# Gates and feature transposes of the last chunks spread among other products, and the last three weight blocks loaded in chained pieces

## What is computed

```python
x = x + attn(layernorm(x))      # z, h~ = projections; h = scan of (1-z) h + z h~ ; gate(h) * h
x = x + xattn(layernorm(x), ctx)  # 16 heads, 77 keys, softmax, Wo
x = x + ffn(layernorm(x))       # experts, below
```

```python
gate_scores = xf @ gate_W + gate_b                 # 4 experts
topk_scores, topk_idx = jax.lax.top_k(gate_scores, 2)
weights = jax.nn.softmax(topk_scores, axis=-1)
# expert e: layernorm2(relu(layernorm1(xf @ W1[e] + b1[e])) @ W2[e] + b2[e])
out = sum_k weights[k] * expert[topk_idx[k]](xf)   # + xf
```

## Time and profile before

| | us |
|---|---|
| timed, median of 3 | 1216.72 |
| timed, lowest and highest | 1214.84, 1219.3 |
| the profiled execution, whole | 1209.59 |
| its span | 1207.8 |

### The profile page before, as it was taken

One profiled execution on the slowest core, in us unless ns is written; L12 is line 12 of the kernel. 1 busy time (PEld: TensorE's weight loads), 2 busy tenths in 40 slices (PEclk: granted clock), 3 DMA queues, 4 the chain that ended last, 5 costly groups with the idle time before them and its releaser, 6 DMA issues.

```text
span 1207.8 us, 24523 instructions
## 1 busy us (share of the span) xinstructions
PE 1159.6 (96%) x6041; PEld 978.9 (81%) x6042; DVE 924.9 (77%) x2196; ACT 731.5 (61%) x2114; POOL 457.2 (38%) x410
## 2 busy tenths in 40 slices
PE   6999999999989999999999998989999999999993
PEld 5788888888878888888888877867888888888882
DVE  6888888887766677877868777678777777777774
ACT  5323333233486757767677662567777777777773
POOL 4040000000052314535445164357655555555543
PEclk9999999999999999999999998899999999999998
DMA  8754544444520302133021358885554444444433
GB/s 271 230 160 160 188 176 146 174 156 165 199 84 1 105 10 97 44 107 104 10 97 44 131 131 227 270 221 122 81 88 81 85 79 86 80 85 80 85 64 42
DMA packets 83237, 143.90 MB, mean 119 GB/s; under 512 B 20460, under 2 KB 24752, under 8 KB 82309
## 3 DMA queue, kind: packets, MB, share of 16 engines
q1 hardware_dynamic: 63872, 101.60, 25.8%
q0 software_dynamic: 18464, 39.14, 17.1%
q10 hardware_dynamic: 837, 2.41, 0.6%
HBM read 78.83 MB, written 67.83 MB: 121 GB/s over the span
## 4 chain that ended last, share of the span: by engine, by line
PE 83%; DMA 5%; DVE 4%; issue 3%; ACT 3%; POOL 2%; POOLq 0%; DVEq 0%; SPq 0%; ACTq 0%
PE banks L1097 27%; PE banks L681 21%; PE banks L746 7%; PE banks L891 6%; PE banks L879 5%; DMA out<-rows,scatter_rows 4%; PE banks L848 3%; PE banks L865 3%; PE banks L1109 2%; PE banks L907 2%; PE banks L1125 2%; ACT rows L1310 2%; PE banks L719 1%; PE banks L800 1%; PE banks L765 1%
## 5 line engine op out<-in xcount | busy, mean ns | idle before, releaser
L1097 PE MATMUL banks<-operands 128*128 x1608 | 388.6, 396 | 10.5 <-DVE operands L1570 5.2
L1097 PEld LDWEIGHTS banks<-operands 128*128 128x128 f32 x1608 | 298.1, 189 | 73.6 <-issue 7.4
L681 PE MATMUL banks<-operands 128*128 128x512 f32 (+2 forms) x1224 | 292.6, 394 | 3.5 <-DVE operands L1570 3.5
L681 PEld LDWEIGHTS banks<-operands 128*128 128x128 f32 (+1 forms) x1224 | 225.6, 192 | 47.8 <-DVE operands L1570 3.7
L1570 DVE TENSOR_TENSOR operands<-banks,operands 128x512 fp32r<-128x512 f32 (+3 forms) x328 | 217.7, 682 | 42.5 <-ACT operands L1189 38.8
L1189 ACT ACTIVATE operands<-banks 128x512 fp32r<-128x512 f32 (+3 forms) x328 | 191.7, 608 | 96.7 <-PE banks L879 45.0
L1310 ACT ACTIVATE rows<-banks,score_shift 128x77 f32<-128x77 f32 x512 | 162.7, 374 | 28.0 <-DVE score_shift L1792 27.2
L1189 ACT ACTIVATE operands<-rows 128x512 fp32r<-128x512 f32 (+3 forms) x79 | 55.3, 709 | 163.8 <-DVE rows L1641 138.1
L1495 ACT ACTIVATE banks<-banks,param_cols 128x128 f32<-128x128 f32 x268 | 99.2, 430 | 82.5 <-PE banks L1125 82.5
L2576 POOL DMA_INDIRECT out<-rows,scatter_rows x67 | 106.6, 1591 | 104.2 <-DVE rows L2315 65.1
L1310 ACT ACTIVATION_READ_ACCUMULATOR rows<-banks,score_shift 128x1 f32 x512 | 129.1, 256 | 0.0
(11 more groups left out here) (178 smaller groups left out, 1707.0 us busy)
## 6 DMA issues: line engine op xcount, KB each, us to landing
expert_parts<-operands SPq DMA_DIRECT2D x32, 512.0 KB, 3.0
operands<-expert_parts SPq DMA_DIRECT2D x8, 2048.0 KB, 11.1
rows<-in_x SPq DMA_DIRECT2D x8, 1024.0 KB, 5.4
rows<-in_L_ffn_W SPq DMA_DIRECT2D x32, 256.0 KB, 3.5
x_rows<-rows SPq DMA_DIRECT2D x8, 1024.0 KB, 4.3
rows<-x_rows SPq DMA_DIRECT2D x8, 1024.0 KB, 5.7
xf_rows<-rows SPq DMA_DIRECT2D x32, 256.0 KB, 2.7
out<-rows SPq DMA_DIRECT2D x32, 256.0 KB, 2.5
```

The lines of the kernel that those rows point to most:

```text
L681: last = nc.tensor.matmul(dst, stationary(a, k), moving(b, k), start=(t == 0 and k == 0), stop=(t == len(terms) - 1 and k == n_k - 1))
L1097: last = nc.tensor.matmul(dst, stationary[:, a, k, :], weights[:, w, bass.ds(e, 1), a2, k, :].rearrange("p e f -> p (e f)"), start=False, ...
```

## The change

On TensorE the gate scores of chunk 6 are cut in three (tile 0, tile 1, tiles 2 and 3) and stand between halves of the first projection of chunk 7; the scores of chunk 7 are cut in two and stand inside `first_product(3)` and `second_product(1)`; the position products move into `first_product(4)`. Both first banks are primed early, and ScalarE fills both at once; banks are given out anew so that this is free. `rows_in` of tile 2 and tile 3 and the transposes of the last two row groups of chunk 7 change places. The routing steps of chunk 7 on VectorE stand one tile later, `plan_early(1)` stands behind `read_positions`, and on GpSimd all eight scatters of chunk 5 stand ahead of `ln3_pow`. On SP block 3 is no longer loaded ahead of the last chunk's stores but together with block 2 behind them; `expert_in(2)` stands behind four pairs of tables; and blocks 5, 6 and 7 are loaded in 16 pieces of 128 KB, each of 64 partitions, every one waiting for the landing of the one before, with tables in between.

```diff
+            PIECES = 4 * KC
+            def load_expert_parts(s, parts):
+                e, w = s // 2, s % 2
+                for n in parts:
+                    a, k, rows = n // (2 * KC), n // 2 % KC, slice(n % 2 * (P // 2), (n % 2 + 1) * (P // 2))
+                    need(sp, w_in[s], 16 * n)
+                    sp.dma_start(weights[rows, w, e, a, k, :].bitcast(F32), ws_d[s, a, k, rows]).then_inc(w_in[s], 16)
...
             load_slot_pairs(3, 5)
-            load_expert(3)
             for j in range(2, TPC):
                 store_base(last - 1, j, slot3(last - 1)[:, j, :])
+            expert_in(1)
...
             load_rows(g2_rows, "L0_ffn_g2", g2_in)
-            expert_in(1)
-            load_slot_pairs(5, 7)
             load_expert(2)
-            load_slot_pairs(7, 9)
+            load_expert(3)
+            load_slot_pairs(5, 9)
             for s in range(2, 5):
                 expert_in(s)
             for s in range(5, 2 * NE):
-                load_expert(s)
-                load_slot_pairs(2 * s - 1, min(2 * s + 1, EARLY // 2))
+                for half_n in range(2):
+                    pair = 2 * s - 1 + half_n
+                    load_expert_parts(s, range(PIECES // 2 * half_n, PIECES // 2 * (half_n + 1)))
+                    load_slot_pairs(pair, min(pair + 1, EARLY // 2))
                 expert_in(s)
...
             last_turn(last)
-            for j in range(TPC):
+            project(last, tail, 0, (0, 1))
+            gate_scores(tail, (1,))
+            project(last, tail, 0, (2, 3))
+            pe.wait_ge(plan_ready, 1)
+            first_experts = [expert_at(pe, i) for i in range(3)]
+            gate_scores(tail, (2, 3))
+            for j in range(1, TPC):
                 project(last, tail, j)
             positions(last - 1, tail, "r")
-            pe.wait_ge(plan_ready, 1)
-            first_product(0, 0, expert_at(pe, 0))
+            first_product(0, 0, first_experts[0])
             for j in range(2):
                 xf_to_features(last, tail, j)
-            pe.wait_ge(mm_read, mm_num(tail, "o3") + 1)
-            prime(m1_bank[1])
-            first_product(1, 1, expert_at(pe, 1))
+            first_product(1, 1, first_experts[1])
+            rows_in(1, 0)
...
+            def prime_and_gates():
+                pe.wait_ge(b_t_read, t_num(tail, "xf3") + 1)
+                prime(m2_bank[1])
+                pe.wait_ge(cx_lo, 4)
+                gate_products(tail_g_bank, tail, range(2))
+            def last_gates():
+                gate_products(tail_g_bank, tail, range(2, TPC)).then_inc(tail_gate_done, 1)
+            def last_positions():
+                pe.wait_ge(route, NROUTE * last_of_b + ROUTE_COUNTED)
+                pe.wait_ge(cx_lo, 5)
+                position_products(tail_r_bank, True).then_inc(tail_pos_done, 1)
```

More of the change, by code:

```diff
@@ L883, in attend, with project @@
                 last.then_inc(mm_done, 1)
-            def project(c, at, j):
-                mm_free(at, f"o{j}")
-                for m in range(KC):
+            def project(c, at, j, parts=range(KC)):
+                if 0 in parts:
+                    mm_free(at, f"o{j}")
+                for m in parts:
                     pe.wait_ge(mm_read, mm_num(c, f"v{m}") + 1)
@@ L914, in gate_scores @@
                     mm_free(at, "g")
-                last = gate_products(mb(at, "g"), at, tiles)
+                last = gate_products(mb(at, "g"), last_of_b if isinstance(at, int) and at == tail else at, tiles)
                 if tiles[-1] == TPC - 1:
@@ L1057, in last_turn @@
                 pe.wait_ge(experts_ready, 1)
-                prime(m1_bank[0])
+                for bank in m1_bank:
+                    prime(bank)
                 rows_in(0, 1)
-                gate_scores(c)
+                gate_scores(tail, (0,))
             pe.wait_ge(consts_done, 1)
@@ L1110, in rows_in, with first_product @@
                 last.then_inc(cx_done, 1)
-            def first_product(i, u, e):
+            def first_product(i, u, e, between=None):
                 pe.wait_ge(experts_ready, 2 * e + 1)
@@ L1155, in c_tile @@
[L1155 to L1157 removed]
+                if early == 0:
+                    pe.wait_ge(mm_read, mm_num(tail, "r") + 1)
+                    prime(m2_bank[0])
+                if early == 2:
+                    pe.wait_ge(tail_gate_read, 1)
+                if early == 3:
+                    pe.wait_ge(tail_pos_read, 1)
+                if after >= 3 and early >= 1:
+                    rows_in(n + 1 + u, 1 - u)
@@ L1158, in c_tile @@
                 experts = coming()
                 if after >= 2:
-                    first_product(i + 2, u, experts[4])
-                second_product(i, u, experts[2], (i + 1, 1 - u) if 1 <= after < 3 else None)
+                    first_product(i + 2, u, experts[4], prime_and_gates if early == 1 else
+                                  last_positions if early == 2 else None)
+                second_product(i, u, experts[2], last_gates if early == 1 else
+                               (lambda: hidden_in(i + 1, 1 - u)) if 1 <= after < 3 else None)
@@ L1526, in c_tile @@
                     hidden(i, experts[2])
+                if early == 2:
+                    route_weights(NCH - 1)
+                if early >= 2:
+                    weighed_be2(*((n, 0) if u else (n - 1, 1)), experts[1])
+                if after >= 1:
+                    hidden_norm(i + 1, 1 - u)
                 if early == 0:
@@ L2386, in _ @@
             x2_rows(last, tail, 0)
+            gate_bias(tail)
+            choose(last - 1, tail)
             count(last - 1)
@@ L2406, in _ @@
             norm_shift(0)
-            for j in range(2, TPC):
-                xf_features(last, tail, j)
+            rows_lo(2, 0)
             statistics(1, 0, m1_bank[1], m1_done, c1_stat)
@@ L2607, in _ @@
             gather(1, 0)
-            for j in range(2):
+            for j in range(TPC):
                 scatter(last - 2, j, aside=1)
             ln3_pow(last, 0)
-            for j in range(2, TPC):
-                scatter(last - 2, j, aside=1)
             gather(1, 1)
```

119 lines of the change are left out of this document (60 added, 59 removed).

## The result

| | us |
|---|---|
| timed before, median of 4 | 1217.97 |
| timed after, median of 4 (1253.72 to 1259.11) | 1256.4 |
| ratio, 95% interval | 1.0319 (1.0286 to 1.0352) |
| profiled span, before and after | 1207.8, 1255.8 |

The change makes the kernel 3.2% slower: 38.4 us, where 7.4 were forecast and 20 was the end of the range. The sign and the place were right, the size wasn't. To a loss of more than 20 us the prediction had given a chance of 0.05. Block 4 was loaded ahead of block 1. Nothing in the sum used it.)

A forecast was written before the change was run, and what follows sets the result against it. TensorE was taken as the bound, busy 1159.6 of 1207.8 us. Late weights in tile 21 absorb the gain: 4.8 us later plus 2.6 low clock, +7.4 on 1216.7, gives 1224 us (1206 to 1237).

The forecast's parts named there:

- The price of a piece: SP's chain for blocks 5, 6 and 7: each of 48 chained 128 KB loads costs 2.8 us (2.3 to 3.2).
- The quiet landing: Lower end for a 128 KB load on a quiet queue: 2.1 us, worked out from 256 KB and 2 MB loads.
- The page of the Trainium skill: Says 64 partitions reach 8 of 16 DMA ports, about half the bandwidth; gave an estimated 2.6 us a piece.
- The late tables: Upper end for a piece: 39 late table loads took 63.17 us, at most 3.2 a pair, amid gathers and adds.
- The end of the chain: Chain for blocks 5, 6 and 7 starts at 778 and ends at 914, or 911.3 with faster last pieces.
- the hastening at the end: While TensorE waits, gathers and adds stop, so the last five or so pieces fall to 2.2 us.
- No wait in tile 19: Block 6, wanted in tile 19 at 880, arrives at 868, so TensorE doesn't wait there.
- The gain of part 1: Clock and waits by tile 3 and after: 17.6 us gross, less 4.6 and 3, net 10 (7 to 13.5).
- add waits: TensorE's waits for low parts of hidden rows in tiles 3, 5, 7: 1.98, 2.29, 0.92 us, removed by small loads.
- The other half: Low clock behind gate rows (6.8) and waits of 1.50 and 2.39 removed, less VectorE steps (4.6) and block 2's wait (3).
- the wait for block 2 in tile 3: At `first_product(5)`, `expert_in(2)` passes at about 778 but is wanted at 775.6: wait of 3 us (0 to 5).
- Rival B: Pieces of 2.43 us or less arrive in time for tile 21, so the gain stays: -10 us, 1206.7; chance 0.18.

The follow-up runs named there:

- e4: Changed kernel with the same 48 chained 128 KB pieces, cut by columns over 128 partitions instead of 64: 1231.74 us, ratio 1.0195 to the kernel before.
- e2: Kernel before with only blocks 5, 6 and 7 loaded in 16 chained 128 KB pieces each, as in the change: 1242.51 us, ratio 1.0278.
- e9: Kernel before with only blocks 5, 6 and 7 loaded in 8 chained 256 KB pieces each, on 128 partitions: 1203.41 us, ratio 0.994.
- e1: Changed kernel with blocks 5, 6 and 7 loaded whole again, one 2 MB transfer each: 1209.18 us, ratio 0.9994 to the kernel before.
- e5: Kernel before, unchanged, profiled once more: 1213.84 us (one run).
- e3: Changed kernel with 24 chained 256 KB pieces on 128 partitions instead of 48 of 128 KB on 64: 1205.73 us, ratio 0.9974 to the kernel before.
- e6: Changed kernel with its 48 pieces on 64 partitions, but two in flight: 1207.7 us, ratio 0.9972 to the kernel before.
- e10: Changed kernel with 24 chained 256 KB pieces, gate products in a row again, `expert_in(2)` ahead of the last two table pairs: 1202.0 us, ratio 0.9941 to the kernel before.

## Why the prediction was wrong, step by step

**The price of a piece: the step that failed.** 2.8 us were forecast (2.3 to 3.2), 2.84 with the tables, and 3.35 measured with them. The mechanism, a sum of 48 landings, was right; its main term was mis-sized. Two parts of it were too small. The quiet landing was read from loads that go to 128 partitions: 2.1, and e4 shows 2.0 for those. But a piece goes to 64, and lands in 2.6 at the least (e2). The row was of another kind of load than the one to be priced, and the sum didn't allow for that. The page of the Trainium skill that has this was weighed beside the sum, and its 2.6 for a piece by itself was set against prices in traffic. By e4 the half width makes 0.37 of the 0.51 us. The second part is the traffic, the other 0.14 over the whole chain: up to 880 a piece took 1.0 to 1.5 us more than the 2.65 of the quiet end, where 0.6 were forecast. The late tables seemed an upper bound of 3.2, but they are two in flight and 1 KB each.

**The end of the chain.** Forecast: 778 + 134 + 2 - 2.7 = 911.3. Measured: 791.3 + 160.9 = 952.2. Of the 40.9 us between, 7.9 is the late M of that execution, 5.3 a later start from M on, 24.9 the pieces and tables, 2.7 the hastening at the end, which did come (2.65 against 3.6 and more) but is in the 160.9. Less the 7.9 this is 33.0. The forecast of +7.4 and the outcome of +39.7 are 32.3 apart. The whole miss is in these terms, because once TensorE waits for the last piece, nothing that comes before counts.

**No wait in tile 19: wrong.** Block 6 was put at 868. It came at 908, by the same price a piece and the same late start, and TensorE waited 11.88 us.

**The gain of part 1, 10 us: hidden, and in part wrong.** It has two halves. The 5.2 us of add waits with the 1.7 of the low clock behind them, 6.9 in all, were right in size (5.7 to 9.4 us between the whole blocks and e9, tiles 4 to 10, and 0.6% of the time in e9), but they go with the chained small loads alone; e9 has them without the moved products, e1 the moved products without them. The other half was 3.1 net: 6.8 of clock and 3.9 of waits, less 4.6 and 3. By the timed ratio of e1 it is worth 0.0006. The low stretches were booked as a fixed cost; that of the gate rows is real but varies, and its removal is paid back by a wait at the position products, which wasn't forecast, and those for VectorE and block 2, which were (4.6 and 3). It would have taken e5, a second profile of the same kernel, to see which of its waits and low stretches are there each time.

**Right:** that the weights of the last expert would bind; the wait for block 2 in tile 3 (2.76 us, 3 forecast), though partly by luck, since the block and the first product that wants it both came some 13 us later than forecast (791.2 against 778, 788.4 against 775.6); 1.8 us of low clock behind each long wait (7.47 us for 24 matmuls against 5.71, 4.80 for 12 against 3.01; 2.6 forecast); that tile 28's table is no limit (from tile 22 to 60 it is 241.3 us in every profile). Rival B, pieces in time, is what e3 and e6 realise, at 3 us of gain and not 10 (e10, with both small edits, at 7).

## What to carry to other kernels

A chain of loads that wait for each other costs its number of landings, and a landing is to be priced in traffic and at the number of partitions that it has here: 3.0 to 3.8 us in this kernel for 128 to 256 KB, almost whatever the size. Cut a background load only as small as its deadline allows (24 pieces ended 26 us ahead of need in e3, 871.9 against 898; with 48 TensorE waited 27 us for the last), and across all partitions. That small chained loads let the foreground's adds through is worth having, and came here from the queue alone. Before a wait or a low-clock stretch of a single profile is booked as a gain, a second profile of the same kernel tells whether it is always there.

## What the runs showed of the hardware that was not expected

- 128 KB to 64 partitions landed in 2.6/3.8 us (least, median), 128 KB to 128 partitions in 2.0/2.9, 256 KB to 128 partitions in 2.5/3.8.
- A chained load of 128 KB to 64 partitions took 3.6 to 4.1 us from issue to issue at a DMA share of 0.67 and still 2.65 at a share of 0.30.
- The same row of 4-column products had a clock of 0.50 behind it in one execution and 1.00 for 10.9 us in another (e5).
- Two executions of the same code reached one point of stage B 3.4 us apart (703.9 and 707.3), and nearly the same code up to 9 us apart.
